# One graph network kernel: two node stages moved into the sum passes that precede them, and a bank zeroed one step sooner

## Time and profile before

| | |
|---|---|
| median of 3 runs | 4441.24 us (4440.9 to 4443.44) |
| the profiled execution | 4441.49 us, its span 4439.7 us |
| PE busy, share of the span | 3201.0 us, 72% |
| DVE | 2591.1 us, 58% |
| ACT | 1319.0 us, 30% |
| POOL | 2128.2 us, 48% |
| mean granted PE clock | 0.795 of full |

### The profile page before, as it was taken

The page is one execution under the profiler, slowest core; times in us unless marked ns, Lnnn a source line. Parts: engine busy times, 40 slices in busy tenths (PEclk is TensorE's granted clock), DMA queues, the critical chain, the costliest instruction groups (busy, mean ns, idle before and its releaser), DMA issues. The chain is left out here.

```text
span 4439.7 us, 76288 instructions
## 1 busy us (share of the span) xinstructions
PE 3201.0 (72%) x18744; PEld 2212.7 (50%) x18758; DVE 2591.1 (58%) x9443; ACT 1319.0 (30%) x2922; POOL 2128.2 (48%) x2166
## 2 busy tenths in 40 slices
PE   2588864667999999289999679999555555555553
PEld 1366652234666666267777457776333333333332
DVE  7688884985555443768887657776632222522223
ACT  0188763940111100245555435555300000100000
POOL 0577771000000000377776167776357777077774
PEclk7599886997999999699999789999755555755555
DMA  2122212000000000366666154545111113422223
GB/s 58 40 70 75 70 64 81 2 5 22 17 16 16 17 12 16 103 180 182 177 182 154 51 153 130 130 129 115 28 56 53 53 53 51 147 53 53 52 53 61
DMA packets 257836, 330.87 MB, mean 75 GB/s; under 512 B 79103, under 2 KB 170062, under 8 KB 256270
## 3 DMA queue, kind: packets, MB, share of 16 engines
q1 hardware_dynamic: 189258, 209.96, 15.4%
q0 software_dynamic: 68256, 117.02, 12.0%
HBM read 232.30 MB, written 94.47 MB: 74 GB/s over the span
## 5 line engine op out<-in xcount | busy, mean ns | idle before, releaser
L2466 PE MATMUL gat_acc<-gat_rows,gat_hot 128*128 128x128 f32 x1664 | 577.2, 479 | 484.3 <-issue 242.9
L925 PE MATMUL hop_p_a<-hop_h,adj 128*128 128x384 bf16 x4375 | 724.6, 328 | 27.2 <-DVE hop_h L866 27.2
L2466 PEld LDWEIGHTS gat_acc<-gat_rows,gat_hot 128*128 128x128 f32 x1664 | 401.1, 317 | 661.7 <-issue 660.9
L925 PEld LDWEIGHTS hop_p_a<-hop_h,adj 128*128 (+1 forms) x4375 | 429.3, 98 | 315.5 <-DVE hop_h L866 34.5
L2450 POOL DMA_INDIRECT gat_rows<-typed_rows,gat_idx x416 | 394.4, 948 | 231.5 <-DVE gat_idx L2473 105.0
L1876 POOL DMA_INDIRECT lb_far<-far_rows,lb_idx x416 | 404.7, 973 | 197.0 <-issue 116.7
L2450 POOL DMA_INDIRECT gat_rows<-hidden_rows,gat_idx x416 | 394.9, 949 | 196.4 <-PE gat_acc L2466 79.8
L1876 POOL DMA_INDIRECT la_far<-far_rows,la_idx x416 | 410.6, 987 | 154.4 <-issue 118.0
L1609 POOL DMA_INDIRECT by_src_records<-scatter_rec,scatter_rank x375 | 384.0, 1024 | 129.0 <-issue 99.4
L2481 DVE TENSOR_SCALAR gat_hot<-iota_row,gat_tabs 128x128 f32<-128x128 f32 x416 | 148.1, 364 | 369.4 <-PE gat_acc L2466 362.8
L534 POOL DMA_INDIRECT mid_by_src_tab_rec<-by_src_records,by_src_off x4 | 4.0, 1002 | 735.1 <-POOLq L81 734.2
(11 more groups left out here) (503 smaller groups left out, 6353.0 us busy)
## 6 DMA issues: line engine op xcount, KB each, us to landing
edge_features<-emb_out SPq DMA_DIRECT2D x104, 256.0 KB
la_feat<-edge_features SPq DMA_DIRECT2D x104, 256.0 KB
edge_features<-la_out SPq DMA_DIRECT2D x104, 256.0 KB
lb_feat<-edge_features SPq DMA_DIRECT2D x104, 256.0 KB
la_place<-dst_row SPq DMA_DIRECT2D x104, 128.0 KB
lb_place<-dst_row SPq DMA_DIRECT2D x104, 128.0 KB
typed_rows<-typed_np_row SPq DMA_DIRECT2D x25, 512.0 KB, 2.7
hop_side<-x0share_nodes SPq DMA_DIRECT2D x125, 64.0 KB
```

Source lines behind the costliest of these rows:

```text
L925: ins = nc.tensor.matmul(p_a[(u.par + r) % 2][:, 0:3 * D], K.adj[:, s, bass.ds(u.t * P, P)], h3[r % 2][:, s, :, :].rearrange("p i d -> p ( ...
L2466: nc.tensor.matmul(acc[:, bass.ds(at[u % LOADS], D)], hot[u % HOTS][:, :], rows[u % RING][:, :], start=False, stop=True, skip_group_check= ...
```

## The change

1. In `adjacency` ACT reads cell c, waits for its own reading to be complete (`s_out`), and zeroes that same bank. The zeroing of cell c-1 after the reading of cell c goes.
2. `gather_pass` takes a function `after` that supplies instructions for each engine behind the pass, in the same phase. The copies to `K.sum` go, and with them two closings of phases.
3. `typed_input` becomes `typed_stage`, run behind the first pass. DVE adds the sums to `K.x` straight from PSUM, a quad at a time. Then quads go through statistics (DVE), norm (ACT), transpose (PE), copy (ACT), product (PE). The product's target is the PSUM of the sums. Of a tile's 1152 columns ACT copies 512 (`low`), DVE copies 512 and adds the bias to the last 128 into `K.h` (`high`). `dr.o` is no longer written. Four row buffers instead of two.
4. `finish` runs behind the second pass: DVE subtracts 1 from `K.x` ahead of the end of the pass, then for each quad adds the sums from PSUM to `K.h`, takes the minimum with 0, and adds the maximum with 0 to `K.x`; ACT takes the exponential; POOL adds it to `K.x`; SP sends the quad out.

```diff
@@ adjacency, ACT @@
                                      accum_out=degs[:, s, w:w + 1]).then_inc(s_out, 1)
-                if c >= 1:
-                    act.wait_ge(s_out, c)
-                    v = (c - 1) % WINS
-                    cols = min(NT * P - v * WIN, WIN)
-                    nc.scalar.activation(acc[:, v * WIN:v * WIN + cols], none[:, 0:cols], ACT.Copy).then_inc(s_zero, 1)
+                act.wait_ge(s_out, c + 1)
+                nc.scalar.activation(acc[:, w * WIN:w * WIN + cols], none[:, 0:cols], ACT.Copy).then_inc(s_zero, 1)
@@ typed_stage, PE @@
+            def turned(q):
+                pe.wait_ge(s_ln, q + 1)
+                if q >= 1:
+                    pe.wait_ge(s_hT, q)
+                for i, t in enumerate(QUADS[q]):
+                    ins = nc.tensor.transpose(p_h[:, i * P:(i + 1) * P], K.h[:, t, :], K.ident[:, :])
+                ins.then_inc(s_hTp, 1)
+            def product(q):
+                pe.wait_ge(s_hT, q + 1)
+                for k, t in enumerate(QUADS[q]):
+                    if t >= 2:
+                        pe.wait_ge(s_low, t - 1)
+                        pe.wait_ge(s_rest, t - 1)
+                    for lo in range(0, (T + 1) * D, 512):
...
+            for r in range(Q + 1):
+                if live(r):
+                    turned(r)
+                if live(r - 1):
+                    product(r - 1)
@@ typed_stage, ACT @@
+            norm(0)
+            for r in range(Q + 1):
+                if live(r):
+                    new_T(r)
+                if live(r + 1):
+                    norm(r + 1)
+                if live(r - 1):
+                    for t in QUADS[r - 1]:
+                        low(t)
@@ typed_stage, DVE @@
+            def high(t):
...
+                nc.vector.tensor_copy(row[t % ROWS][:, 512:T * D], p_o[t % 2][:, 512:T * D]).then_inc(s_high, 1)
+                nc.vector.tensor_tensor(K.h[:, t, :], p_o[t % 2][:, T * D:(T + 1) * D], b[:, :], ALU.add).then_inc(s_rest, 1)
+            roots(0)
+            for r in range(Q + 1):
+                if live(r + 1):
+                    roots(r + 1)
+                if live(r - 1):
+                    for t in QUADS[r - 1]:
+                        high(t)
@@ finish, DVE @@
+            nc.vector.tensor_scalar(K.x[:, :, :], K.x[:, :, :], 1.0, None, ALU.subtract).then_inc(s_less, 1)
+            dve.wait_ge(s_less, 1)
+            dve.wait_ge(s_sum, U)
+            for q in range(Q):
+                n = width(q) * D
+                nc.vector.tensor_tensor(nodes(K.h, q), acc[:, 512 * q:512 * q + n].rearrange("p (t d) -> p t d", d=D),
+                                        nodes(K.h, q), ALU.add).then_inc(s_o, 1)
+                dve.wait_ge(s_o, q + 1)
+                if q >= 2:
+                    dve.wait_ge(s_x, q - 1)
+                nc.vector.tensor_scalar(e[q % 2][:, 0:width(q), :], nodes(K.h, q), 0.0, None, ALU.min).then_inc(s_m, 1)
+                nc.vector.scalar_tensor_tensor(nodes(K.x, q), nodes(K.h, q), 0.0, nodes(K.x, q), ALU.max, ALU.add)\
+                    .then_inc(s_r, 1)
@@ finish, POOL @@
+                nc.gpsimd.tensor_tensor(nodes(K.x, q), nodes(K.x, q), e[q % 2][:, 0:width(q), :], ALU.add).then_inc(s_x, 1)
```

More of the change, by code:

```diff
@@ L2413, in node_update, with gather_pass @@
     ph.close()
-def gather_pass(nc, K, lay, table, cols):
+def gather_pass(nc, K, lay, table, cols, after):
     ph = Phase(nc, f"gat{lay.key}")
@@ L2434, in gather_pass @@
     s_rows = [ph.sem(f"rows{i}") for i in range(RING)]
-    HALF = 3 * BANK
+    end = after(ph, acc, s_sum, U)
     with ph.block() as block:
@@ L2440, in _ @@
             sp.dma_start(tile_row[:, :], lay.tiles).then_inc(s_tab, 16)
+            end.sync(sp)
         @block.gpsimd
@@ L2452, in _ @@
                     .then_inc(s_rows[u % RING], 16)
+            end.gpsimd(pool)
         @block.tensor
@@ L2483, in _ @@
                 ins.then_inc(s_hot, 1)
[L2484 to L2486 removed]
+            end.vector(dve)
         @block.scalar
         def _(act):
[L2490 to L2491 removed]
+            end.scalar(act)
@@ L2492, in gather_pass @@
     ph.close()
[L2495 to L2508, removed]
-            for t in range(T):
[L2510 to L2530, removed]
@@ L2533, in finish @@
-def finish(nc, A, K, dr, out):
[L2535 to L2567, removed]
@@ new lines, in finish, with parts, sync, gpsimd @@
+def finish(nc, A, K, dr, out):
+    def parts(ph, acc, s_sum, U):
+        Q = len(QUADS)
+        e = [ph.sb(f"fin_e{i}", [P, 4, D]) for i in range(2)]
+        s_less, s_o, s_m, s_e, s_r, s_x, s_out = (ph.sem("fin_" + x) for x in ("less", "o", "clipped", "exp", "rest", "x", "out"))
+        width = lambda q: len(QUADS[q])
+        nodes = lambda t, q: t[:, 4 * q:4 * q + width(q), :]
+        end = Parts()
+        def sync(sp):
+            for q in range(Q):
+                sp.wait_ge(s_x, q + 1)
+                if q < Q - 1:
+                    sp.dma_start(out[4 * q * P:(4 * q + 4) * P, :].rearrange("(t p) d -> p t d", p=P), nodes(K.x, q))\
+                      .then_inc(s_out, 16)
+                else:
+                    sp.dma_start(out[(NT - 1) * P:N, :], K.x[0:NLAST, NT - 1, :]).then_inc(s_out, 16)
+            sp.wait_ge(s_out, Q * 16)
+        def gpsimd(pool):
+            for q in range(Q):
+                pool.wait_ge(s_e, q + 1)
+                pool.wait_ge(s_r, q + 1)
+                nc.gpsimd.tensor_tensor(nodes(K.x, q), nodes(K.x, q), e[q % 2][:, 0:width(q), :], ALU.add).then_inc(s_x, 1)
+        def tensor(pe):
+            pass
+        def scalar(act):
+            for q in range(Q):
+                act.wait_ge(s_m, q + 1)
+                nc.scalar.activation(e[q % 2][:, 0:width(q), :], e[q % 2][:, 0:width(q), :], ACT.Exp).then_inc(s_e, 1)
+        def vector(dve):
+            nc.vector.tensor_scalar(K.x[:, :, :], K.x[:, :, :], 1.0, None, ALU.subtract).then_inc(s_less, 1)
+            dve.wait_ge(s_less, 1)
+            dve.wait_ge(s_sum, U)
+            for q in range(Q):
+                n = width(q) * D
+                nc.vector.tensor_tensor(nodes(K.h, q), acc[:, 512 * q:512 * q + n].rearrange("p (t d) -> p t d", d=D),
+                                        nodes(K.h, q), ALU.add).then_inc(s_o, 1)
+                dve.wait_ge(s_o, q + 1)
+                if q >= 2:
+                    dve.wait_ge(s_x, q - 1)
+                nc.vector.tensor_scalar(e[q % 2][:, 0:width(q), :], nodes(K.h, q), 0.0, None, ALU.min).then_inc(s_m, 1)
+                nc.vector.scalar_tensor_tensor(nodes(K.x, q), nodes(K.h, q), 0.0, nodes(K.x, q), ALU.max, ALU.add)\
+                    .then_inc(s_r, 1)
+        end.sync, end.gpsimd, end.tensor, end.scalar, end.vector = sync, gpsimd, tensor, scalar, vector
+        return end
+    return parts
```

93 lines of the change are left out of this document (89 added, 4 removed).

## The result

The changed kernel takes 4421.84 us (median of 5, 4417.09 to 4423.01), the kernel before 4441.24 us beside it (median of 5, 4439.21 to 4445.52). The ratio is 0.9954, with a 95% interval from 0.9941 to 0.9968, and the medians lie 19.4 us apart: a small gain, but clear of the noise. The forecast was 4416.4 us, range 4407 to 4429. The profiled execution took 4420.16 us, its span is 4418.4.

The account below looks back on a forecast made before the run. DVE was taken to bound the adjacency, POOL's indirect DMAs the sum passes, latency the two tails. Terms +1 - 5 - 21.0 + 0.2 = -24.8 gave 4416.4 us; own range 4411 to 4421, 8-in-10 range 4407 to 4429.

Parts of the forecast that it names:

- Part 1: Adjacency, zeroing each bank at once: gains nothing, costs +1 us, from 0 to +10.
- the lag: Adjacency: ACT falls back 0.14 us behind DVE per row of cells, 3.5 us over 25 rows.
- the 3.4 us of slack: Adjacency: ring of six cells, 6.7 us, less about 2 for POOL's block reads and 1.3 for reading and zeroing.
- Part 2: Between the passes, pipeline by quads: -5 us, between -11 (no clock drop) and -1 (longest drops).
- the loop: Between the passes: eviction, roots, norm and `low` hold PE before third tiles; 11.3 us a quad against 8.2 of PE work.
- the spells: Between the passes: PE's 3.0 us gaps bring its clock to 1.2 GHz, costing +6 us in all.
- The two of three: Between the passes: two of three gaps cost about 3 us each, a slow stretch closing the next gap.
- Part 3: Last sum to the end, final arithmetic by quads: -21.0 us, bounds -19 to -22.5.
- A small store and a closing, 3.5 from its issue: The end: from the last store's issue to the end of the span takes 3.5 us, ending at 4418.7.
- the 0.43 for the minimum: The end: DVE's minimum takes 0.43 us beside POOL, within 1.76 us of DVE per quad.
- the rival to which I gave 0.05: The end: POOL and DVE wait for each other fully, 1.5 us per quad, +9, total 4425.5; chance 0.05.
- ACT's wait in the adjacency: Rival: ACT's self-wait costs 0.05 to 0.1 us more than 0.04, +10 to +17, total 4425 to 4433; chance 0.15.

Follow-up runs that it names:

- run 1: Changed kernel with the old zeroing order (cell c-1 after reading cell c): adjacency 242.4 us, against 246.5 in the kernels beside it.
- Run 4: Changed kernel with DVE's roots in two groups (tiles 0 to 7, 8 to 24) ahead of the first eviction: 71.5 us between the passes, 11.8 less.
- run 8: Changed kernel with two unread PE products ahead of the third tile's wait in quads 1 to 3: 80.5 us between the passes, against 83.3.
- run 2: Changed kernel with POOL's final add moved to DVE, one quad later: 19.2 us from last sum to end, against 24.5.
- run 10: Changed kernel with old zeroing order, roots in two groups, min(exp, 1) added by DVE and POOL idle: 4396.9 us, ratio 0.9902 to the kernel before.
- run 3: Changed kernel with the final add on DVE and POOL waiting for DVE's last add before the closing: 23.7 us from last sum to end, against 24.5.
- run 5: Changed kernel with the final stage's minimum as a two-input instruction (adding zeros): last store 17.4 us after the last sum, a quad 2.57 us.
- run 6: Changed kernel with sums plus h kept in PSUM at the end and read there: last store 13.6 us after the last sum, a quad 1.93 us.

## Why the prediction was right and wrong

**Part 1: right in its mechanism, mis-sized in its slack.** ACT's wide cell is 1.24 us (forecast 1.23) with the 0.04 taken from DVE, and run 1 shows that the wait is the cause. Two terms of the sum were too kind. By the start of ACT's readings of the first and the 25th row of cells, counted from the first memset, a row took (203.76 - 11.20) / 24 = 8.02 us and before, at DVE's pace, (199.11 - 11.29) / 24 = 7.83, so the lag is 0.19 a row and not 0.14: 4.7 us and not 3.5. And of the 3.4 us of slack that I set against it, an estimate from one pair of events, less than 1 was there at the end: ACT's last row came 4.7 us late and DVE's last groups 3.9. DVE kept its old pace up to the 70th of 114 groups, and of what it lost behind that 2.2 us fell on a single group, the 95th, whose wait is shown above.

**Part 2: the loop as forecast, the spells too dear.** First product 14.1 us after the last sum (14.7 forecast); gaps of 2.6 (3.0) ahead of the third tile of quads 1 to 3, filled by `roots`, `norm` and `low` in that order; bare loop 11.06 (11.3). Run 4 shows the loop by taking it away. The clock fell after two gaps of three, as said, but for 3.4 us each, which cost 1.7 us, not 3: 3.4 in all where I took 6 (83.3 against run 8's 80.5 says 2.8). I had sized it from spells of up to 10.2 us in another stage. With that -9.0 instead of -5, inside the bounds. Run 8 puts the stage without spells at 80.5, so -11.8 where I had said -11.0. The two of three held in all seven executions of this loop, but not for my reason, that a slow stretch closes the next gap: all three gaps are 2.6 us, and in four of the seven the spells follow the first two. So the number was luck, and what lets one gap pass is not known.

**Part 3: wrong, and outside its bounds.** The step that failed is the last: "A small store and a closing, 3.5 from its issue", which took 8.8. I read the closing's price from the earlier trace rows, a phase in which POOL has nothing to do. There the DRAIN takes 0.03 us. In a pass it takes 15.6, and in the kernel before it ran from 4389.9 to 4405.5, hidden behind the last fetches, the last sums and the copies but for its last 0.7 us (DVE was done with them at 4404.8). The change put POOL's adds ahead of it and so moved the whole DRAIN, 8.6 us of it by then, behind the arithmetic. Even without it the 3.5 was short: runs 2 and 10, where the DRAIN is long over, take 4.3 and 4.4 us from the last store to the end. The second error is the 0.43 for the minimum "(beside POOL)". The row that I took it from, 1850.25 in the earlier trace rows, is of a minimum that had started 0.06 us *before* POOL's add; it was POOL that waited there (1.50 instead of 1.26). Here POOL comes first. That is +3.1 us to the last store (15.7 instead of 12.6): the rival to which I gave 0.05, at a third of its price, because only one of DVE's three instructions meets the add. 5.3 + 3.1 = 8.4 us, against 8.3 by the table: the whole miss from -21.0 to -12.7.

**The total** fell into the range in part by luck. In the profiled execution +2.7 on part 1 and +8.3 on part 3 met -4.0 on part 2 and -3.3 ahead of the change, which no part of the forecast explains. Against the median I was 5.4 us too low; that the range reached up to 4429 covers it, but it had been widened on that side for ACT's wait in the adjacency and not for the end.

## What to carry to other kernels

When work moves onto an engine's queue behind its last transfer, look at what that engine does at the closing: a DRAIN that used to run under other work may now stand at the end, and the view of the closing's own line shows it where the chain of waits names another engine. Where two engines keep each other out, read them in the order in which they start: a row in which the short instruction came first says nothing on the case in which it comes second. And put the serial chain (here the roots) ahead of a loop whose buffers turn on the same engine, rather than into it.

## What the runs showed of the hardware

- POOL's DRAIN at the closing of a pass takes 12.4 to 15.8 us over the passes in the traces when it starts with the last fetches still to run, and 8.5 to 11.7 us of that lie behind the end of the last fetch. It still takes 8.1 to 9.0 us when it starts 19 to 25 us after the last fetch has started, even if POOL did nothing since (run 3, 8.06). In `typed_input` of the kernel before, where POOL has no work, it takes 0.03. The profile counts it as no work and books the wait on PE's sequencer.
- A gap of 2.6 us in PE's work does not always bring the clock down: of the three in the loop between the passes two did, in each of seven executions, for 3.4 us each; the first and the second in four of them (the changed kernel and its repetition, runs 2 and 5), the first and the third in three (runs 1, 3 and 6). With gaps of 0.9 the clock stayed at 1.00 in both runs. In the adjacency the nine gaps of 2.27 us, one in each trace with zeroing at once, all did, and those of 1.3 to 1.7 us ahead of them never.
- A DVE instruction with its inputs in SBUF that starts under POOL's add ends 0.29 us (0.43 us long alone) or 0.55 us (0.69 alone) after that add: about 0.14 us of it overlaps, the rest waits. Where DVE starts first, by 0.06 us in the earlier trace rows, POOL's add waits instead (1.50 us instead of 1.26).
